# The second bias of a graph convolution: from a matmul per turn to the bias operand of a ScalarE copy

## What is computed

```python
def gcn_conv(x, edge_index, W, b):
    h = x @ W
    coef = dinv[src] * dinv[dst]
    agg = segment_sum(h[src] * coef[:, None], dst)
    agg = agg + h * (dinv * dinv)[:, None]
    return agg + b

h = relu(gcn_conv(x, edge_index, W1, b1))        # 64 -> 128
y = gcn_conv(h, edge_index, W2, b2)              # 128 -> 64
x = layernorm(x + y)
```

## Time and profile before

| | |
|---|---|
| time, median of 3 runs | 4774.9 us (4772.15 to 4782.6) |
| the profiled execution: time | 4780.41 us |
| the profiled execution: span | 4778.7 us |
| granted PE clock, mean over the span | 0.884 |
| PE busy over the span | 4088.1 us (86%) |
| DVE busy | 3215.4 us (67%) |
| ACT busy | 1960.7 us (41%) |
| the own stage | about 249 to 858 us |

### The profile page before, as it was taken

One profiled execution on the slowest core, in us unless ns is written; L12 is line 12 of the kernel. 1 busy time (PEld: TensorE's weight loads), 2 busy tenths in 40 slices (PEclk: granted clock), 3 DMA queues, 4 the chain that ended last, 5 costly groups with the idle time before them and its releaser, 6 DMA issues. The chain is left out here.

```text
span 4778.7 us, 78736 instructions
## 1 busy us (share of the span) xinstructions
PE 4088.1 (86%) x24119; PEld 2923.4 (61%) x24119; DVE 3215.4 (67%) x7115; ACT 1960.7 (41%) x3684; POOL 2801.5 (59%) x2859
## 2 busy tenths in 40 slices
PE   5989999799989999778996899898998666777776
PEld 1278888688877777668884555555555344444443
DVE  9967777667667888767776688888888433333332
ACT  0056666344444445324342155555555222222222
POOL 0066665576656666577762545455550377777777
PEclk9989999899999999855555989999998799888888
DMA  1089998799986676545543444444442222222221
GB/s 40 1 256 286 287 287 270 196 230 230 229 216 171 191 191 188 139 95 136 133 114 86 109 104 110 107 112 107 113 110 53 67 66 66 55 66 67 55 65 29
DMA packets 1127654, 649.03 MB, mean 136 GB/s; under 512 B 908912, under 2 KB 944313, under 8 KB 1127240
## 3 DMA queue, kind: packets, MB, share of 16 engines
q1 hardware_dynamic: 1039432, 555.85, 42.4%
q0 software_dynamic: 87808, 88.16, 9.3%
HBM read 384.70 MB, written 261.63 MB: 135 GB/s over the span
## 5 line engine op out<-in xcount | busy, mean ns | idle before, releaser
L2237 POOL DMA_INDIRECT r_got<-x_table,slot_idx x392 | 409.9, 1046 | 568.5 <-DVE r_masked L2470 340.0
L1089 POOL DMA_INDIRECT o_rows<-in_x_dram,dst_idx x392 | 369.9, 944 | 444.8 <-POOLq L348 242.0
L2552 POOL DMA_INDIRECT m_rows<-x_table,slot_idx x392 | 376.2, 960 | 223.9 <-issue 118.8
L2691 DVE TENSOR_TENSOR_SCAN m_both<-m_keep,m_both,m_rows_t 128x512 f32<-128x512 bf16 x97 | 124.1, 1280 | 545.2 <-PE m_rows_t L2614 545.2
L1541 POOL DMA_INDIRECT b_rows<-h_table,slot_idx x392 | 369.7, 943 | 206.9 <-issue 91.5
L1352 POOL DMA_INDIRECT a_got<-node_table,src_idx x392 | 375.5, 958 | 194.9 <-DVE a_conv L1488 57.4
L2336 PE MATMUL r_source_t<-r_masked,rel_pair 64*128 64x512 f32 x980 | 470.9, 626 | 0.0
L2338 PE MATMUL r_own_t<-r_masked,rel_pair 64*128 64x512 f32 x980 | 470.8, 626 | 0.0
L2560 POOL DMA_INDIRECT out_dram<-s_res,put_out x392 | 390.5, 996 | 135.7 <-issue 109.8
L2010 POOL DMA_INDIRECT t_got<-x_table,slot_idx x392 | 377.5, 963 | 144.8 <-issue 101.2
L2470 DVE SCALAR_TENSOR_TENSOR r_masked<-r_half,r_both_t 128x512 f32<-128x512 bf16 x490 | 301.0, 678 | 68.3 <-PE r_both_t L2321 68.2
(11 more groups left out here) (401 smaller groups left out, 11785.3 us busy)
## 6 DMA issues: line engine op xcount, KB each, us to landing
x_table<-n_res SPq DMA_DIRECT2D x196, 256.0 KB
n_rows<-x_table SPq DMA_DIRECT2D x196, 256.0 KB
x_table<-s_res SPq DMA_DIRECT2D x294, 128.0 KB
node_table<-n_wide SPq DMA_DIRECT2D x98, 272.0 KB, 3.9
h_table<-n_conv SPq DMA_DIRECT2D x98, 256.0 KB
x_table<-s_res SPq DMA_DIRECT2D x98, 256.0 KB
r_feats<-in_edge_attr_dram SPq DMA_DIRECT2D x390, 64.0 KB
n_rows<-in_x_dram SPq DMA_DIRECT2D x97, 256.0 KB
```

The source lines that it names most:

```text
L1089: nc.gpsimd.indirect_dma_start(out=rows[:, n % 4, t, :], out_offset=None, in_=x, in_offset=bass.IndirectOffsetOnAxis(ap=dst_idx[:, n * TIL ...
L2237: nc.gpsimd.indirect_dma_start(out=got[:, n % RING, t, :], out_offset=None, in_=x2_table, in_offset=bass.IndirectOffsetOnAxis(ap=slot_idx[ ...
L2552: nc.gpsimd.indirect_dma_start(out=rows[:, n % 4, t, 0:D], out_offset=None, in_=x3_table, in_offset=bass.IndirectOffsetOnAxis(ap=slot_idx[ ...
```

## The change

The bias matmul L942 goes, once per turn. In its place ACT's copy of the turned rows adds `b2` as it writes `n_turned_s`: it becomes an activation `Identity` with a bias operand `b2_two`, which holds `b2` twice, one value per partition. The centring of x + `b2` is then done by the matmul that centres x. Since `project` reads the same `n_turned_s`, its product has now `W1` transposed times `b2` in it; the preparation takes this out of `b1_col` beforehand, with one small matmul and one subtraction. The second layer's copy stays as it was.

```diff
-    b2_wide = sb(ctx, "b2_wide", [P, ROWS, D], BF16)
+    b2_two = sb(ctx, "b2_two", [P, 1])
...
-        WEIGHT_LOADS = 36
+        WEIGHT_LOADS = 38
...
-                for wide in (b2_wide, res_wide, out_wide, ub2_wide):
+                for wide in (res_wide, out_wide, ub2_wide):
                     vec.memset(wide[:, :, :], 0.0).then_inc(*v.one())
...
                 dve.wait_ge(tensor_steps, W2T_TURNED)
+                vec.tensor_tensor(b1_col[:, :], b1_col[:, :], made_t[1][:, 384:385], ALU.subtract).then_inc(*v.one())
...
-                for wide, at, many, width in ((b2_wide, V_B2, ROWS, D), (res_wide, V_RES, ROWS, D), (out_wide, V_OUT, TILES, D),
+                for wide, at, many, width in ((res_wide, V_RES, ROWS, D), (out_wide, V_OUT, TILES, D),
...
                     (w1_2[0:D, :], ins["L0_gnn_W1"]), (w1_2[D:P, :], ins["L0_gnn_W1"]),
+                    (b2_two[0:D, :], column(ins["L0_gnn_b2"])), (b2_two[D:P, :], column(ins["L0_gnn_b2"])),
...
                 pe.wait_ge(weights_in, 16 * WEIGHT_LOADS)
+                nc.tensor.matmul(made_t[1][:, 384:385], w1_2[0:D, :], b2_two[0:D, :], start=True, stop=True)
...
             if self.gcn:
-                nc.tensor.matmul(to[:, :], ones3[:, :], b2_wide[:, :, :].rearrange("k j d -> k (j d)"), start=False, stop=False,
-                                 skip_group_check=True)
                 for q in range(ROWS // 2):
...
+            if self.gcn:
+                nc.scalar.activation(self.turned_s[:, n % 4, :], self.turned_t[:, :], ACT.Identity, bias=b2_two[:, 0:1]).then_inc(self.copied[n], 1)
+                return
             nc.scalar.activation(self.turned_s[:, n % 4, :], self.turned_t[:, :], ACT.Copy).then_inc(self.copied[n], 1)
```

## The result

| | before | changed |
|---|---|---|
| time, median of 4 runs | 4778.45 us | 4757.36 us (4750.53 to 4758.8) |
| ratio, with its 95% interval | | 0.9954 (0.9937 to 0.9971) |
| the profiled execution: time | 4780.41 us | 4756.46 us |
| the profiled execution: span | 4778.7 us | 4754.7 us |
| steady turn of the own stage | 6.03 us | 5.82 us |

The kernel is 21.1 us faster by the medians, against 21.4 forecast. As a time it is 4757.4 us against 4753.5 forecast: the median before, with its fourth run, stands 3.6 us above the 4774.9 from which the forecast was counted. The first view is busy time by stretch in the own stage of the changed kernel; the last three columns are the granted clock, the share of the DMA engines and GB/s. It answers to the earlier trace rows.

What follows compares the result with a forecast made beforehand. PE's unbroken instruction sequence was taken to bound the own stage. Removing 98 bias matmuls (21.3 us) plus 0.1 us of preparation gave 21.4 us off the 4774.9 us median: 4753.5 us, range 4747 to 4765.

Steps and rivals of the forecast that it cites:

- PE's sequence sets the turn: Own stage: PE's back-to-back instructions make the 6.03 us turn; without the bias matmul it takes 5.81 us.
- The bias matmul is worth the distance of starts, 0.215 us: PE, own stage: each removed matmul saves its start-to-start distance, not 0.38 us busy; 21.3 us over 98 turns.
- The rival by which part of its place stays: PE, L945's first weight load: 0.08 us per turn comes into the open; gain 13 us, time 4762 us; chance 0.08.
- The seam that I feared between transposition and f32 product: PE: the new neighbours might cost at most 0.04 us at half clock, some 0.02 at full clock.
- The dearer copy costs nothing: ACT's changed copy takes 0.09 us more per turn, hidden because PE's sequence stays longer by 0.17 us.
- The term for its room: ACT and DVE circle: 5.64 us with the dearer copy against PE's 5.81, leaving about 0.17 us ahead of `n_hidden`.
- The third rival's middle case: ACT becomes the bound: a copy dearer by 0.35 us leaves half the gain, 4765 us; whole rival's chance 0.03.
- What is late next: ACT's wait for PE ahead of `n_hidden` should shrink from 0.48 to about 0.17 us per turn.
- a slack of 0.43 us: PE's `sum_up` waits for `n_conv`: 0.74 us of slack, less the 0.31 by which ACT's chain moves, leaves 0.43.
- DMA: Own stage: DMA share rises to 0.976; rival that transfers become the bound, 4766 or 4775 us, chance 0.08.
- The preparation: Before the stages: added loads and matmul hidden, DVE subtraction costs about 0.15 us, dropped copy frees 0.21; together -0.1 us.
- The sum: Whole kernel: 21.3 us from the bias matmul plus 0.1 from the preparation, 21.4 us saved.

Runs made afterwards that it cites:

- e4: Kernel before, with the bias matmul issued twice in a row per turn; ratio 1.0045, turn 6.25 us.
- e1: Kernel before, with the bias matmul left out and ACT's copy kept plain; ratio 0.9963, own stage 589.5 us.
- e2: Kernel before, bias matmul kept, ACT's copy made Identity with a bias column of zeros; ratio 1.0001, turn 6.03 us.
- e3: Changed kernel with one extra 128x512 ACT copy per turn into a spare tile; ratio 0.9995, turn 6.015 us.
- e7: Changed kernel with one extra half-width (128x256) ACT copy per turn; ratio 0.9963, turn 5.816 us.
- e5: Changed kernel with the second layer's bias matmul of the own stage also left out; ratio 0.9932, turn 5.63 us.
- e6: Changed kernel storing 128 KB more per turn in the own stage, to a table nobody reads; ratio 0.9964, turn 5.81 us.
- e9: e5 with seven more reciprocals in the preparation, so that stages start later; ratio 0.9969, own stage 571.8 us.
- e10: Changed kernel with four more reciprocals in the preparation, so that stages start later; ratio 0.9995, own stage 589.4 us.
- e0: The changed kernel as it is, timed again; ratio 0.9957, median 4756.29 us.
- e8: Changed kernel with two extra full-width 128x512 ACT copies per turn; ratio 1.0093, turn 6.50 us.

## Why the prediction was right

- **PE's sequence sets the turn.** Right. The turn went from 6.03 to 5.816 us, forecast 5.81 to 5.82, and e4 shows the same 21 us with the opposite sign.
- **The bias matmul is worth the distance of starts, 0.215 us.** Right, by e4's timeline and by the turn. The rival by which part of its place stays is refuted: the 0.08 us of the weight load did not come into the open, and the turn fell by 0.213 us where the rival had 0.135. The seam that I feared between transposition and f32 product is not there: 0.44 us to the next instruction in both kernels. The Trainium skill, page "TensorE: Matmul & The Clock Gate", section "Back-to-back issue gap", gives a sustained 131 ns for a matmul of 512 columns and about 216 ns for one by itself. The trace agrees with the second, 0.215 us, also for the two equal matmuls of e4 in a row; with the first the turn would have been 5.90 us and not 5.816.
- **The dearer copy costs nothing.** Right: +0.09 us (0.59 to 0.68) as bounded from two relus, and e1 and e2 separate it from the matmul. The term for its room was mis-sized. "So the circle of ACT and DVE alone would take 6.03 - 0.48 = 5.55 us a turn, with the dearer copy 5.64" took the idle column for the room; the runs e3 and e7 put the circle with the dearer copy at 5.55, so without it at 5.46. The room left is 0.27 us and not 0.17, and the point from which ACT makes the kernel slower than before lies 0.57 and not 0.48 us above the old copy. The third rival's middle case, a copy dearer by 0.35 us, would by this have cost nothing. It changed nothing in the sum.
- **What is late next.** Named in part. The prediction took the circle of ACT and DVE for the next bound and the wait of `sum_up` for `n_conv` for a slack of 0.43 us. That slack is as long as forecast, but it belongs to the circle of two turns through PE, and at 5.63 us a turn, by e5, that one comes before the circle of ACT and DVE at 5.55.
- **DMA.** The share came to 0.98, forecast 0.976, and the rival failed: e6 had 7.5% more bytes in the same turn.
- **The preparation.** Forecast -0.1 us; the own stage starts 0.8 us earlier in this profile. But the start was anywhere from 248.6 to 249.8 us in the profiles of kernels with the changed preparation (without e9 and e10), and 249.6, 249.6, 249.0 and 248.7 in those with the old one (before, e1, e2, e4). A tenth of a microsecond can't be told there. The two steps themselves are as read: the added subtraction took 0.07 us of DVE (its row starts at 53.30, the next at 53.37), where 0.15 was put.
- **The sum.** 21.3 us were for the own stage and 20.0 came: 98 x 0.213 is 20.9, PE's idle time for the first load of the next stage grew from 16.94 to 17.41 us, and some 0.4 remain. The medians differ by 21.1 us, the profiled executions by 24.0, of which 3.2 lie in stages that both kernels share. That the total came within 0.3 us of 21.4 is luck: its parts don't fit that closely, and the intervals allow some 8 us. The sign of being wrong by a later stage that changes by more than 5 us was too narrow: none did in the first profile, but e0, the same kernel again, has a relation stage 7.6 us shorter than before.

## What to carry to other kernels

Where an engine has no pauses, price its instructions by the distance from start to start and not by busy time, and an edit is worth that distance times the turns until the next circle of engines becomes the bound. Find that next circle beforehand, and measure its room likewise, from start to start: the idle column understates it by the overlap of neighbours. A circle may also run through the engine that sets the pace now, and take more than one turn; list for each wait of that engine how long before it what it waits for is ready. An additive vector that enters through a matmul of its own can, as here, ride in a copy that is made anyway, if what else reads that copy is corrected once.

## What the runs showed of the hardware

The share of the DMA engines is not bounded by 1: in e6 it stood at 1.03 to 1.05 for hundreds of microseconds without one engine waiting for a landing. A share near 1 alone is no evidence that transfers set the pace.

The clock at a stage's start can go up, down and up again. Before, PE ran at 1.2 GHz (0.50) up to 265 us and then at 2.4 GHz. In e2, whose instructions there differ by one copy's form, it had the full level from about 257 to 267 us, half from about 268 to 277, and the full one for good by 279. Busy time by stretch, first before, then e2; the third number from the end is the granted clock, the number behind the comma PE's busy time:

```profile
255.00:265.00 10.00, 9.83 (x37) 7.07 (x36) 2.39 (x7) 5.01 (x8) 7.56 (x9) 0.50 0.92 295
265.00:275.00 10.00, 10.00 (x74) 8.15 (x74) 5.86 (x14) 5.64 (x10) 7.56 (x9) 0.97 0.81 210
275.00:285.00 10.00, 10.00 (x77) 8.24 (x76) 6.41 (x14) 6.62 (x13) 7.56 (x9) 1.00 1.00 288
```

```profile
255.00:265.00 10.00, 9.71 (x63) 7.10 (x61) 2.08 (x6) 5.35 (x8) 7.55 (x9) 0.90 0.92 287
265.00:275.00 10.00, 7.13 (x29) 5.85 (x29) 6.19 (x16) 3.30 (x6) 7.56 (x9) 0.61 0.87 242
275.00:285.00 10.00, 10.00 (x71) 8.58 (x69) 3.62 (x8) 6.92 (x12) 7.56 (x9) 0.88 0.70 188
```

Ahead of the fall PE stood idle. At the higher clock it had run ahead of what it needs, and waited for DVE:

```profile
267.87 0.61 PE L944 MATMUL n_sum_t<-b_wide,ones 128*128 128x512 bf16 x1 [2.98 <-DVE n_conv L1043]
```

The profiled executions of e2 and e4 had this, and own stages 3 to 4 us longer than their turns explain. In e7 and e8 the full level also came early, at about 256 to 257 us, and PE waited for `n_conv` too (1.59 us in e7, until 265.82), but the clock stayed at 1.00; e7 has the shortest own stage of all with a turn of 5.82 us. So what made it fall in two of the four is open. In the other kernels it rose once in the stage, at 264 to 266 us, in e10 and e9 with their later starts at 276 and 282, and stayed. It is a matter of some microseconds at a stage's start, not of the change: e2's ratio is 1.0001.
